# Three streamed attentions and one absorbed attention on one core: the query path moved to ScalarE's DMA queue, and the unit order of layer 3 changed

## The reference, cut to what matters

```python
x = x + xattn(layernorm(x), ctx)   # 16 heads, 12544 keys
x = x + attn(layernorm(x))
x = x + ffn(layernorm(x))

# xattn of layers 0 to 2, head dim 16
q = split_heads(x @ Wq + bq); k = split_heads(y @ Wk + bk); v = split_heads(y @ Wv + bv)
weights = softmax(q @ k.T / sqrt(16))
out = merge_heads(weights @ v) @ Wo + bo
# xattn of layer 3: the same with head dim 64, low-rank additions to Wq, Wk, Wv, Wo, and 4 keys in a softmax of their own
```

## Time and profile before

| | |
|---|---|
| median of 3 runs | 3316.8 us (3313.58 to 3319.33) |
| the profiled execution | 3317.55 us, span 3315.8 us |
| TensorE busy | 2940.3 us (89%), mean granted clock 0.913 |
| DVE, ACT, POOL busy | 1830.3, 1350.1, 402.9 us |
| DMA | 393.95 MB, mean 119 GB/s |
| starts of the three streamed stages | 390, 926 and 1442 us |
| units of layer 3 | 2048 to 3133 us |

### The profile page before, as it was taken

How to read it: one execution, slowest core, us unless ns; L and a number is a source line. 1 busy time by engine, 2 the same in 40 slices (tenths; PEclk the granted TensorE clock), 3 DMA queues, 4 the chain that set the end, 5 groups by cost and what they waited for, 6 DMA issues and landing times. The chain is left out here.

```text
span 3315.8 us, 66524 instructions
## 1 busy us (share of the span) xinstructions
PE 2940.3 (89%) x27158; PEld 2482.7 (75%) x27158; DVE 1830.3 (55%) x3246; ACT 1350.1 (41%) x2191; POOL 402.9 (12%) x571
## 2 busy tenths in 40 slices
PE   7999669995959997659998769999999999999978
PEld 6998537773827775636776646999999999999867
DVE  5556357774247773548774434555555555555424
ACT  4555226672106664215665111444443444444311
POOL 2444300001000000000000004020202020100000
PEclk9999869997959997879998766999999999999969
DMA  5888688851868880369882351110101010000016
GB/s 157 301 322 332 264 174 176 177 120 51 283 131 169 175 177 26 122 166 180 176 176 55 136 164 39 40 40 1 40 1 40 1 40 1 1 1 1 17 52 230
DMA packets 204581, 393.95 MB, mean 119 GB/s; under 512 B 33491, under 2 KB 164948, under 8 KB 201588
## 3 DMA queue, kind: packets, MB, share of 16 engines
q1 hardware_dynamic: 202599, 388.90, 43.9%
q10 hardware_dynamic: 1680, 0.80, 0.1%
HBM read 289.45 MB, written 99.49 MB: 117 GB/s over the span
## 5 line engine op out<-in xcount | busy, mean ns | idle before, releaser
L729 DVE TENSOR_REDUCE L_xattn_tops<-psum 128x1 f32<-128x896 f32 x672 | 702.4, 1086 | 272.4 <-PE psum L591 271.1
L652 ACT ACTIVATE L_xattn_probs<-psum 128x512 f32<-128x512 f32 x1176 | 612.1, 601 | 483.1 <-PE psum L602 483.1
L1737 DVE TENSOR_TENSOR L_units_low<-psum,L_units_high 128x896 fp32r<-128x896 f32 x224 | 243.6, 1087 | 486.1 <-ACT L_units_high L1686 486.1
L591 PE MATMUL psum<-L_xattn_keys,L_xattn_q_stack 96*128 96x448 bf16 (+1 forms) x1344 | 394.8, 378 | 113.0 <-DMA L_xattn_q_stack<-query_parts 66.0
L1654 PE MATMUL psum<-wide_tokens,L_units_high 128*128 128x386 f32 x1568 | 455.8, 359 | 1.4 <-DVE L_units_low L1737 1.4
L602 PEld LDWEIGHTS psum<-L_xattn_q_stack,L_xattn_keys 99*128 99x128 bf16 (+1 forms) x4704 | 322.3, 98 | 143.9 <-issue 18.6
L602 PE MATMUL psum<-L_xattn_q_stack,L_xattn_keys 99*128 99x128 bf16 (+1 forms) x4704 | 393.3, 221 | 5.0 <-ACT L_xattn_probs L652 5.0
L1655 PE MATMUL psum<-wide_tokens,L_units_low 128*128 128x194 f32 x1568 | 394.5, 252 | 0.0
L615 PE MATMUL psum<-L_xattn_probs,L_xattn_values 128*17 128x128 f32 x9408 | 357.0, 276 | 0.4 <-ACT L_xattn_probs L652 0.2
L1686 ACT CAST L_units_high<-psum 128x896 fp32r<-128x896 f32 x224 | 203.1, 907 | 363.5 <-PE psum L1642 363.5
L1678 ACT ACTIVATE L_units_raw<-L_units_raw,L_units_negmax 128x896 f32<-128x896 f32 x224 | 221.5, 1036 | 307.6 <-DVE L_units_negmax L1728 307.6
(11 more groups left out here) (436 smaller groups left out, 3985.9 us busy)
## 6 DMA issues: line engine op xcount, KB each, us to landing
key_parts<-proj_parts SPq DMA_DIRECT2D x84, 672.0 KB, 4.2
L_xattn_keys<-key_parts SPq DMA_DIRECT2D x144, 336.0 KB, 4.7
values_scratch<-proj_values SPq DMA_DIRECT2D x21, 1904.0 KB, 7.9
L_xattn_values<-values_scratch SPq DMA_DIRECT2D x144, 238.0 KB, 5.2
L_ffn_w<-in_L_ffn_W SPq DMA_DIRECT2D x32, 1024.0 KB, 6.8
L_xattn_keys<-key_parts SPq DMA_DIRECT2D x144, 224.0 KB, 5.0
L_xattn_keys<-key_parts SPq DMA_DIRECT2D x192, 112.0 KB, 5.0
L_ffn_w<-in_L_ffn_w SPq DMA_DIRECT2D x16, 1024.0 KB, 6.9
```

Of the source, the lines that this page charges most:

```text
L591: last = pe.matmul(top_slot(n)[:, s, :], q_stack[0:P1, h, :], keys[0:P1, v % RING, key:key + WIN // 2], start=True, stop=True)
L652: act.activation(group_probs(k), score_bank(k), ACT.Exp).then_inc(sem("probs"), 1)
L729: dve.tensor_reduce(tops[:, h % 2, 2 * c + w:2 * c + w + 1], top_slot(n), AX.XY, ALU.max)\
L1737: dve.tensor_tensor(low[gr][:], turned_banks(gr), high[gr][:], ALU.subtract).then_inc(sem("low"), 1)
```

## The change

It touches four places. In `setup`, SP also writes `ones_bf` to a new DRAM row `ones_row`. In the streamed stage, ACT's queue loads `wq` and `bq`, writes `qparts` in one DMA, and reads back three of the six blocks of `q_stack`; SP's queue issues one pair of fills, reads back the other three blocks, waits for the whole stack, and then issues the other fills. The ones rows of `keys` come from `ones_row`; in layers 1 and 2 they are issued behind head 0's fills and awaited by the first scores, in layer 0 they stay ahead of the fills. In layer 3 the orders of TensorE and DVE in a unit change.

```diff
@@ -160,7 +160,10 @@
         @block.sync
         def _(sp):
             sp.dma_start(g.x[:], a["x"].rearrange("b t d -> (b t) d")).then_inc(st.sem("x"), 16)
-            sp.wait_ge(st.sem("x"), 16)
+            sp.wait_ge(st.sem("ones_bf"), 1)
+            sp.dma_start(dram(g.ones_row, 0, [[128, NK // 128], [1, 128]]), g.ones_bf[0:NK // 128, :])\
+              .then_inc(st.sem("x"), 16)
+            sp.wait_ge(st.sem("x"), 32)
 
         @block.gpsimd
         def _(pool):
@@ -175,7 +178,7 @@
         @block.vector
         def _(dve):
             dve.memset(g.ones[:], 1.0)
-            dve.memset(g.ones_bf[:], 1.0)
+            dve.memset(g.ones_bf[:], 1.0).then_inc(st.sem("ones_bf"), 1)
             dve.wait_ge(st.sem("band"), 1)
             dve.tensor_copy(g.ident_bf[:], g.ident)
 
@@ -510,6 +513,15 @@
             sum_bank = bank(g, 7, 0, T)
             gathered = bank(g, 2, 0, H * VW)
 
+            def stack_rows(eng, at, copies, part):
+                src = dram(g.query_parts, part * D * T, [[T, HD], [HD * T, H], [1, T]])
+                eng.dma_start(q_stack[at * HD + part:(at + copies) * HD:copies, :, :], src)\
+                   .then_inc(sem("stack"), 16)
+
+            def ones_rows(eng):
+                eng.dma_start(keys[SEG:SEG + 3, :, :], dram(g.ones_row, 0, [[0, 3], [0, RING], [1, CH]]))\
+                   .then_inc(sem("key_rows"), 16)
+
             @block.sync
             def _(sp):
                 def fill(h, j):
@@ -525,42 +537,30 @@
                     sp.dma_start(values[:, slot:slot + n, :, :].rearrange("p n t e -> p n (t e)"), src)\
                       .then_inc(landed, 16)
 
-                sp.dma_start(wq[:], a[f"{name}_Wq"].rearrange("(k p) n -> p k n", p=128)).then_inc(sem("wq"), 16)
-                if biased:
-                    for k in range(DG):
-                        sp.dma_start(bq[:, k:k + 1], dram(a[f"{name}_bq"], 128 * k, [[1, 128], [1, 1]]))\
-                          .then_inc(sem("wq"), 16)
                 if masked:
                     for r in range(PARTS_RING):
                         sp.wait_ge(g.drain.sem(f"parts_out{r}"), 16 * 2 * NCH)
                     for r in range(2):
                         sp.wait_ge(g.drain.sem(f"values_out{r}"), 16 * 3 * len(range(r, NCH, 2)))
                     sp.wait_ge(g.drain.sem("mask_out"), 16)
-                sp.dma_start(keys[SEG:SEG + 3, :, :].rearrange("p s (n t) -> p (s n) t", t=128),
-                             g.ones_bf[0:3, :].unsqueeze(1).to_broadcast([3, RING * TPC, 128]))\
-                  .then_inc(sem("key_rows"), 16)
-                for j in range(len(PAIRS)):
-                    fill(0, j)
                 if masked:
+                    ones_rows(sp)
                     for p in range(DEEP):
                         sp.dma_start(keys[SEG + 3:SEG + 4, p * NCH:p * NCH + NCH, :],
-                                     dram(g.mask_row, 0, [[NK, 1], [CH, NCH], [1, CH]])).then_inc(sem("key_rows"), 16)
-
-                sp.wait_ge(sem("qparts"), 1)
-                for part in range(3):
-                    sp.dma_start(dram(g.query_parts, part * D * T, [[T, 128], [128 * T, DG], [1, T]]),
-                                 qparts[:, part, :, :]).then_inc(sem("qparts_out"), 16)
-                sp.wait_ge(sem("qparts_out"), 48)
-                for at, copies in ((0, 3), (3, 2), (5, 1)):
-                    for part in range(copies):
-                        src = dram(g.query_parts, part * D * T, [[T, HD], [HD * T, H], [1, T]])
-                        sp.dma_start(q_stack[at * HD + part:(at + copies) * HD:copies, :, :], src)\
-                          .then_inc(sem("stack"), 16)
-                if masked:
+                                     dram(g.mask_row, 0, [[NK, 1], [CH, NCH], [1, CH]])).then_inc(sem("mask_rows"), 16)
                     sp.wait_ge(sem("stack_zero"), 1)
                     sp.dma_start(q_stack[SEG + 3:SEG + 4, :, :],
                                  g.ones_bf[0:1, :].unsqueeze(1).to_broadcast([1, H, T]))\
                       .then_inc(sem("stack"), 16)
+                fill(0, 0)
+                sp.wait_ge(sem("qparts_out"), 16)
+                for part in range(3):
+                    stack_rows(sp, 0, 3, part)
+                sp.wait_ge(sem("stack"), STACK)
+                for j in range(1, len(PAIRS)):
+                    fill(0, j)
+                if not masked:
+                    ones_rows(sp)
                 for h in range(1, H):
                     for j, (c, n) in enumerate(PAIRS):
                         if h >= DEEP:
@@ -578,7 +578,9 @@
                                          start=(j == 0), stop=(j == DG - 1))
                 last.then_inc(sem("q_in_psum"), 1)
                 pe.wait_ge(sem("stack"), STACK)
-                pe.wait_ge(sem("key_rows"), 16 * (1 + DEEP) if masked else 16)
+                if masked:
+                    pe.wait_ge(sem("key_rows"), 16)
+                    pe.wait_ge(sem("mask_rows"), 16 * DEEP)
                 pe.wait_ge(sem("q"), 1)
 
                 def top(v, w):
@@ -595,6 +597,8 @@
                 def scores(k):
                     h = (k * GROUP + GROUP - 1) // (NCH * TPC)
                     pe.wait_ge(sem("shifted"), 4 * (h + 1))
+                    if k == 0:
+                        pe.wait_ge(sem("key_rows"), 16)
                     at_least(pe, sem("probs"), k - 2)
                     for i in range(GROUP):
                         tile = k * GROUP + i
@@ -646,6 +650,19 @@
 
             @block.scalar
             def _(act):
+                act.dma_start(wq[:], a[f"{name}_Wq"].rearrange("(k p) n -> p k n", p=128)).then_inc(sem("wq"), 16)
+                if biased:
+                    for k in range(DG):
+                        act.dma_start(bq[:, k:k + 1], dram(a[f"{name}_bq"], 128 * k, [[1, 128], [1, 1]]))\
+                           .then_inc(sem("wq"), 16)
+                act.wait_ge(sem("qparts"), 1)
+                act.dma_start(dram(g.query_parts, 0, [[T, 128], [D * T, 3], [128 * T, DG], [1, T]]), qparts[:])\
+                   .then_inc(sem("qparts_out"), 16)
+                act.wait_ge(sem("qparts_out"), 16)
+                for part in range(2):
+                    stack_rows(act, 3, 2, part)
+                stack_rows(act, 5, 1, 0)
+
                 def exp(k):
                     act.wait_ge(sem("scores"), k + 1)
                     at_least(act, sem("sums"), -(-(k * GROUP + GROUP - HELD) // TPC))
@@ -1659,11 +1676,11 @@
             for s in range(4):
                 raw_scores(0, s)
             for u in range(NU):
-                for gr in range(2):
-                    turn(u, gr)
-                    if u + 1 < NU:
-                        raw_scores(u + 1, 2 * gr)
-                        raw_scores(u + 1, 2 * gr + 1)
+                turn(u, 0)
+                turn(u, 1)
+                if u + 1 < NU:
+                    for s in range(4):
+                        raw_scores(u + 1, s)
                 sums(u, 0)
                 sums(u, 1)
 
@@ -1753,15 +1770,19 @@
                 keep(0, s)
             new_max(0)
             for u in range(NU):
-                for gr in range(2):
-                    keep_low(u, gr)
-                    if u + 1 < NU:
-                        keep(u + 1, 2 * gr)
-                        keep(u + 1, 2 * gr + 1)
-                    if gr == 0 and u > 0:
-                        take(u - 1)
-                if u + 1 < NU:
+                ahead = u + 1 < NU
+                if ahead:
+                    keep(u + 1, 0)
+                    keep(u + 1, 1)
+                keep_low(u, 0)
+                if ahead:
+                    keep(u + 1, 2)
+                keep_low(u, 1)
+                if ahead:
+                    keep(u + 1, 3)
                     new_max(u + 1)
+                if u > 0:
+                    take(u - 1)
             take(NU - 1)
 
 
@@ -2835,6 +2856,7 @@
         g.values = nc.dram_tensor("values_scratch", (3, NCH, 128, H, TPC * VW), F32, kind="Internal").ap()
         g.query_parts = nc.dram_tensor("query_parts", (3, D, T), BF16, kind="Internal").ap()
         g.mask_row = nc.dram_tensor("mask_row", (1, NK), BF16, kind="Internal").ap()
+        g.ones_row = nc.dram_tensor("ones_row", (1, NK), BF16, kind="Internal").ap()
         g.acc, g.neg_all = sb("acc", [T, H, VW]), sb("neg_all", [T, H])
         run = {name for name in ORDER} if stages is None else set(stages)
         setup(nc, g, a)
```

## The result

Four runs of the changed kernel took 3274.86 to 3288.04 us, median 3285.55, beside 3318.07 for the kernel before: a ratio of 0.990 with a 95% interval of 0.9885 to 0.9914. It is faster by 32.5 us where 66 were forecast, and lies 12.5 us above the range.

A forecast was written before the change was run, and what follows sets the result against it. TensorE idles 35 to 50 us at three streamed starts; in layer 3 only waits between matmuls can be won. Gains 22.4 + 14.9 + 14.0 + 15 - 0.3 = 66.0 off 3317.55, median 0.75 lower: 3250.8 us, range 3230 to 3273.

The forecast's parts named there:

- The query chain, first tops of layers 1 and 2: Start of layers 1 and 2: first top matmul at t = 17.4, sooner by 21.4 us in layer 1, 20.5 in layer 2.
- the small loads: Weights and biases on ScalarE's queue beside the first pair: query matmuls delayed 3.0 us, from t = 3.56 to 6.6.
- rival 4: Streamed starts: the query write still meets fills; only issue time (5.8) and layer 3 remain, 3296 us; chance 0.03.
- the ones rows at 3.9 us: Layers 1 and 2, between heads 0 and 1: 75 KB per engine on three engines makes later fills 3.9 us later.
- the 2.6 for late fills: Streamed starts: fills held until the stack put first scores at S + 24.8 instead of S + 22.2, giving back 2.6 us.
- Rival 1: Streamed starts: the lead starves, a pair takes 4.9 us and the ones 5.9, total 3264 us; chance 0.15.
- Nothing else holds the stage, so a top that comes sooner ends it sooner: Streamed stages, told for layer 2: an earlier first top matmul was claimed to bring the stage's end earlier; no separate size.
- Layer 0's first top, S = 419: Start of layer 0: first top at 419, 25 us before 444.06; 22.4 gained after 2.6 for the fills.
- Layer 3, 15 us: Layer 3's units: new order removes waits, 0.12 up to 0.15 us per unit, times 111, taken as 15 us.
- Rivals 2 and 5: Layer 3: 2, sums wait for keep_low, no gain, 3266, chance 0.12; 5, keep_low stalls every unit, 3387, chance 0.05.
- Setup, 0.3: Setup: writing the ones row to DRAM beside the load of x costs 0.3 us (0 to 1).
- more than forecast: Streamed starts, rival 3: small loads not delayed, ones rows cost nothing, 17.7 us more gain, 3233; chance 0.13.

The follow-up runs named there:

- rows by head: Full change, but in layers 1 and 2 head 0's ones rows go out behind the first pair, the others behind head 2's fills: 3281.53 us, ratio 0.9891.
- by memset: Full change, but in layers 1 and 2 GpSimd writes the ones rows with a memset and no DMA does: 3293.55 us, ratio 0.9924.
- by ScalarE: Full change, but in layers 1 and 2 ScalarE writes the ones rows in one copy behind its read-back issues: 3275.27 us, ratio 0.9877.
- the spread transfer: Kernel with head 0's ones rows early, plus a dummy transfer of the same 225,792 bytes into 128 partitions at the ones rows' old place: 3283.71 us, ratio 0.9896.
- The last kernel: Two pairs of fills ahead in layers 1 and 2, added to the combined kernel with ScalarE's rows, layer 0's split rows and no read-back wait: 3251.06 us, ratio 0.9802.
- The kernel with a third of the rows: Full change, but in layer 0 only head 0's ones and mask rows precede the first pair, later heads' rows precede their fills: 3278.48 us, ratio 0.988.
- the half alone: Kernel before the change with layer 3's new order and nothing else: 3299.33 us, ratio 0.995.
- the streamed half alone: Full change with layer 3's old order: 3304.13 us, ratio 0.996.
- the kernel without the wait for the read-backs: Kernel with ScalarE's ones rows and layer 0's rows split by head, without SyncE's read-back wait before pairs 1 to 3: 3260.69 us, ratio 0.9825.

## Why the prediction was wrong, point by point

**The query chain, first tops of layers 1 and 2: right.** Forecast 17.4 us after the start in layer 1 and 17.3 in layer 2, measured 18.4 and 18.9. Of the 1.0 and 1.6 missing, 0.8 in layer 2 are the small loads, which delayed the query matmuls to t = 7.4 instead of 6.6. From the first read-back issue to the first top there went 4.8 us instead of 3.8, and the write gave 0.6 back (2.3 us instead of 2.9). The write met an empty queue; rival 4 is out.

**The step that failed most: the ones rows at 3.9 us.** The prediction took them as 75 KB on each of three DMA engines, at 19 GB/s per engine, and let the fills pass on the others. With the 2.6 for late fills that made first scores 28.7 us behind the first top; they came at 35.6 and 36.7. Taken out of that place they give 8.5 and 9.6 us back (the kernels with rows by head, by memset and by ScalarE agree: 26.0 to 27.3), so the term is 9 us and not 3.9. What is left, 26.0 to 27.3 instead of 24.8, is the late fills at 4 to 5 us and not 2.6; in layer 2 the window of pair 1 could start only 7.9 us after the first top, where its pair was to land after 6.1.

Three engines was right, and two things about them were wrong. The first is the rate. In layer 0 no fill is under way yet when the ones rows start: there the pieces, three at a time, take 0.14 us each in the first rounds and then 0.44, so that the three engines together move 24 GB/s, not three times 19. The row that the 19 came from the earlier trace rows wasn't the mask rows alone either: their last piece ends at 437.0, and the rest of that window is the query write. The second is that the fills don't pass: their pieces take twice as long beside the ones rows. The source plays no part, and the bytes alone cost 0.7 us on average, so the rest hangs on the narrow shape. The Trainium skill (SBUF — State Buffer, Door 1: The DMA port swizzle) has partitions 64–67 and 96–99 on one of sixteen ports, of about 27 GB/s; by it 226 KB need 8.3 us, an estimate, and rows 96 to 98 stand in the way of every fill's rows 64 to 67. The measured 9 us and the 24 GB/s agree, and so does the small cost of the spread transfer; no run here moved the rows to another port, so the port as the cause is not shown. Rival 1 had this shape (ones 5.9, a slower pair) at a chance of 0.15 and still priced it too low.

**"Nothing else holds the stage, so a top that comes sooner ends it sooner": only half right.** With the rows by head, first scores 8.5 and 9.6 us sooner brought the ends of layers 1 and 2 only 0.3 and 3.1 sooner. TensorE now stands still behind the first scores, 11 to 31 us after them. In the twelve profiled kernels with the new query path this happens 55 times for over 0.5 us. Two of these idle times end with a landing of ones rows, one with a fill, and one behind DVE. For the other 51 the profile names nothing. 44 of them stand in the middle of a group of matmuls, often at the same place in different kernels (in layer 1 between the 12th and the 13th of 28 sums). And each of the 51 ends 1.3 to 1.8 us after the end of a packet of 16,384 bytes on this queue of the page after:

```profile
q8 instruction: 217, 3.56, 0.5%
```

By their kind these packets load the program's own instructions. So TensorE waited there for its instructions, a wait that the prediction didn't have. With the old query path (the kernel before, and that with layer 3's order alone) there is no such idle time in six stages.

Why the packets come too late is argued and not shown. The ring holds 21 slots of 0.466 MB, 9.8 MB, which at 205 GB/s are 48 us. Before, most of that had landed when the first scores came, 61 us after the start of layer 1. A window of the kernel before, 5 us behind its first scores:

```profile
992.00:997.00 5.00, 5.00 (x67) 3.42 (x69) 2.85 (x3) 2.13 (x5) 0.00 (x0) 0.63 0.62 139
```

Now the first scores come 42 to 56 us after the start, the fills of the ring are still under way, and the DMA share stays above 1 where TensorE stops (1.12 and 1.07 in layer 2 of the full change and of the kernel with ScalarE's rows). An instruction packet then has more traffic beside it. The last kernel fits this: with one pair more landed in idle time these stops fall from 4.4 to 2.1 us in layer 1 and from 2.9 us to none in layer 2. No run changed the traffic and nothing else. In layer 0 the full change already paid: 304.2 us behind the first scores instead of 299.8, with 3.2 us of such stops. The term varies between runs: the same code of layer 0 took 304.2 to 309.2 in seven profiles.

**Layer 0's first top, S = 419: 5.8 us too early.** In its own frame 25 us sooner were forecast and 18.0 came. The path was right: one engine carries a ones row, the mask rows and its share of the pair, and it ends last. The sum had it free at 417.9, and it was free at 419.8: the ones pieces on it lasted until 412.6, since the three slow each other and everything else (82 to 115 GB/s from 408 to 414). The larger error is what came then. The sum let the write pass and only 0.9 us of read-backs stand at the end; the write's last pieces were on that same engine, so it landed at 420.1, and the whole of the read-backs, 4.6 us to the first top, followed. The kernel with a third of the rows shows it: 6.1 us for the write. The Trainium skill's rule against this move (DMA: Bandwidth & Descriptors, Issuing engines are not separate DMA queues: DMAs of all issuers run on the same engines and interleave) is borne out here: the pieces of ScalarE's write took turns with those of SyncE's rows on the last engine, and didn't get past them.

**Layer 3, 15 us: right.** 0.15 us per unit by the windows is 16 us for 111 units, and the half alone measured 17.5 (12 to 21 by its interval). Rivals 2 and 5 are out: the sums wait for nothing, keep_low of half 0 starts 2.84 us after the unit's first raw matmul where 2.75 were forecast.

**Setup, 0.3: less.** The next stage's first transfer is issued at 3.87 us instead of 3.83.

**The account.** Forecast for the three attentions 51.3, measured by the table 21.4. (By the typical run it is less: the streamed half alone measured 12.7.) The 29.9 missing in the profile are, within rounding: first scores behind the first top, 14.9 in layers 1 and 2 and 0.6 in layer 0; layer 0's first top 7.0; the other first tops 2.6; behind the first scores 4.7. The chances had 0.13 on more than forecast and 0.15 on the starved lead; the two unknown costs, ones rows and fills, were bounded apart (0 to 11.7 for the ones), and the range did not take in both at once with layer 0's.

## What to carry to other kernels

Moving a chain of dependent steps ahead of bulk transfers wins only what the bulk can still deliver: count all bytes that must land until the steady state, at the measured rate, and fill the idle time of the chain with as many of them as land before the chain's first transfer (here two pairs, not one). When a transfer is only a few partitions high, look at GB/s against the DMA share, not at the share alone; if such rows are constant, an idle engine can write them. When an engine stops in the middle of a group that has no wait, look at the instruction packets before calling it a wait for data. And a change early in a stage shows its price at the end of the stage, so compare whole stages.

## What was unexpected of the hardware

- A transfer of 226 KB into three neighbouring partitions, carried by three engines, halves the rate of all transfers beside it for about 10 us (232 down to 91 to 158 GB/s at a share near 1); as 128 partitions the same bytes do nothing of the kind (218 and 257).
- TensorE can run out of instructions: 51 idle times of 0.6 to 4.5 us in the streamed stages each end 1.3 to 1.8 us after the end of an instruction packet, all with the new query path and none before.
- A GpSimd memset of 15.77 us held DVE's cast from fp32 to bf16 for 8.10 us instead of 0.29. The Trainium skill (SBUF — State Buffer, Who interferes with whom) says that such a cast and a GpSimd operation can want the same pair of ports, and that the first to issue holds it for its whole instruction; this trace agrees. ScalarE's copy of the same 3 x 18816 words (15.87 us) held nobody.
- An idle time of 3.63 us is followed by half clock (0.79 and 0.53 in the windows of the kernel without the wait for the read-backs): a unit's 28 sums took 1.90 and 1.47 us behind it and 1.06 ahead of it, so that it costs more than its length.
